# Conditioning vectors of the second layer: five of ten formed behind the expert slots, their weights loaded during the slots

## The reference

```
mod = silu(c) @ wmod                      # c: 4 x 512, wmod: 512 x (6*512)
sa, ca, ga, sb, cb, gb = six parts of mod, each 4 x 512
ga, gb = sign(g) * max(|g|, 0.25)
x = x + ga * attn(layernorm(x) * (1 + ca) + sa)
x = x + gb * ffn (layernorm(x) * (1 + cb) + sb)
```

## Time and profile before

| | us |
|---|---|
| median of 3 runs (1924.27 to 1926.55) | 1926.1 |
| the profiled execution, its own time | 1928.25 |
| its span, first to last instruction | 1925.8 |
| TensorE busy in the span | 1798.4 (93%) |
| VectorE | 1179.9 (61%) |
| ScalarE | 754.3 (39%) |
| GpSimd | 688.0 (36%) |
| chain that ended last: TensorE, VectorE, DMA, GpSimd | 68%, 12%, 6%, 3% |

### The profile page before, as it was taken

The page is one execution under the profiler, slowest core; times in us unless marked ns, Lnnn a source line. Parts: engine busy times, 40 slices in busy tenths (PEclk is TensorE's granted clock), DMA queues, the critical chain, the costliest instruction groups (busy, mean ns, idle before and its releaser), DMA issues.

```text
span 1925.8 us, 25658 instructions
## 1 busy us (share of the span) xinstructions
PE 1798.4 (93%) x8308; PEld 1406.5 (73%) x8308; DVE 1179.9 (61%) x2152; ACT 754.3 (39%) x1465; POOL 688.0 (36%) x678
## 2 busy tenths in 40 slices
PE   8889999999999999998799999679799999999995
PEld 5556788888888888876566777468688787787784
DVE  5556676666666766677763344556557466575654
ACT  2534455554555555543622222266622213222120
POOL 1335222112222212211253556634536436344442
PEclk9999999999999999999989999889999999999998
DMA  6122353535352544622377998710001101001011
GB/s 246 45 91 82 119 160 92 177 109 197 100 191 81 169 137 142 203 74 75 132 247 216 277 276 222 155 70 26 23 24 50 33 6 55 27 9 51 6 55 44
DMA packets 99905, 216.33 MB, mean 112 GB/s; under 512 B 8456, under 2 KB 33048, under 8 KB 98288
## 3 DMA queue, kind: packets, MB, share of 16 engines
q1 hardware_dynamic: 77696, 166.60, 26.6%
q0 software_dynamic: 11520, 28.96, 6.4%
q10 hardware_dynamic: 10608, 19.74, 3.3%
HBM read 123.93 MB, written 91.35 MB: 112 GB/s over the span
## 4 chain that ended last, share of the span: by engine, by line
PE 68%; DVE 12%; issue 7%; DMA 6%; POOL 3%; ACT 3%; POOLq 0%; ACTq 0%; DVEq 0%; SPq 0%
PE bank L770 19%; PE bank L772 18%; PE bank L771 18%; DMA u_d<-yt,sm 4%; PE bank L1011 2%; PE bank L874 2%; PE bank L1156 2%; DVE hh L2219 2%; PE bank L957 2%; DMA gbt<-mod_rows_d,sm 1%; POOL gbt L2450 1%; DVE rr L1906 1%; PE bank L1018 1%; DVE fl L2197 1%; PE bank L959 1%
## 5 line engine op out<-in xcount | busy, mean ns | idle before, releaser
L1906 DVE RECIPROCAL rr<-rr 128x256 f32<-128x256 f32 x128 | 218.9, 1731 | 0.0
L770 PE MATMUL bank<-hT,W1b 128*128 128x512 f32 x512 | 208.0, 406 | 7.5 <-DVE hh L2172 7.5
L770 PE MATMUL bank<-W1a,hT 128*128 128x512 f32 x512 | 209.8, 410 | 3.4 <-DVE hT L1818 3.4
L771 PE MATMUL bank<-hT,W1b 128*128 128x512 f32 x512 | 203.3, 397 | 0.0
L772 PE MATMUL bank<-hT,W1b 128*128 128x512 f32 x512 | 203.1, 397 | 0.0
L772 PE MATMUL bank<-W1a,hT 128*128 128x512 f32 x512 | 201.5, 394 | 0.0
L771 PE MATMUL bank<-W1a,hT 128*128 128x512 f32 x512 | 200.7, 392 | 0.0
L2305 POOL TENSOR_TENSOR x<-x,tmp 128x512 f32<-128x512 f32 x64 | 101.3, 1583 | 271.5 <-DVE tmp L1898 271.5
L2172 DVE TENSOR_TENSOR hh<-hh,bank 128x512 f32<-128x512 f32 x64 | 43.4, 687 | 196.5 <-PE bank L772 168.5
L1931 DVE SCALAR_TENSOR_TENSOR kt<-bank,kt 128x256 fp32r<-128x256 f32 x128 | 50.8, 397 | 162.4 <-ACT vt L1373 162.2
L2239 POOL TENSOR_TENSOR W<-stage,W 128x1024 fp32r<-128x1024 f32 x32 | 77.1, 2408 | 184.5 <-ACT W L1235 182.2
(11 more groups left out here) (272 smaller groups left out, 4467.4 us busy)
## 6 DMA issues: line engine op xcount, KB each, us to landing
hs_d<-bor SPq DMA_DIRECT2D x24, 1548.0 KB, 11.1
ws_d<-W SPq DMA_DIRECT2D x48, 512.0 KB, 6.1
WB<-ws_d SPq DMA_DIRECT2D x8, 3072.0 KB
stage<-wa SPq DMA_DIRECT2D x32, 512.0 KB
stage<-wbe SPq DMA_DIRECT2D x24, 512.0 KB
stage<-wdn SPq DMA_DIRECT2D x24, 512.0 KB
mw<-wmod SPq DMA_DIRECT2D x10, 1024.0 KB, 4.8
hg<-hs_d ACTq DMA_DIRECT2D x39, 258.0 KB
```

The lines of the kernel that those rows point to most:

```text
L770: pe.matmul(o, lhs(HI), rhs(HI), start=start, stop=False, **kw)
L771: pe.matmul(o, lhs(HI), rhs(LO), start=False, stop=False, **kw)
L1906: dve.reciprocal(rr[:, pair, h], rr[:, pair, h]).then_inc(r_rec, 1)
```

## The change

Parts 5 to 9 of `MOD_PARTS` leave the first head group, with their loads, products, copies, column groups and the last gate. Their weights get a buffer of their own, `lw`, of 5 x 2048 words from word 6144 on: its first two parts lie ahead of WB, the last three in WB's first buffer. SP issues the five loads behind that of the last expert, the last three of them after the last slot of expert 5. After the last slot TensorE forms the products in five free banks, ScalarE copies the rows and the columns (between and behind the diagonals), and GpSimd makes and stores the gate in step b=0 of stage C. ScalarE's scaling of (2, 1) goes behind the output of (2, 0).

```diff
-MOD_PARTS = [(0, GAT), (0, SB), (0, CB), (0, GBT), (1, GAT), (1, SA), (1, CA), (1, SB), (1, CB), (1, GBT)]
-MOD_FINISH = [(0,), (3,), (4,), (9,)]
-MOD_PLACE = [(0, 0), (0, 1), (0, 2), (1, 0), (1, 2), (2, 0), (2, 1), (2, 2), (3, 0), (3, 2)]
+MOD_PARTS = [(0, GAT), (0, SB), (0, CB), (0, GBT), (1, GAT)]
+MOD_FINISH = [(0,), (3,), (4,), ()]
+MOD_PLACE = [(0, 0), (0, 1), (0, 2), (1, 0), (1, 2)]
+LATE_PARTS, LATE_ROW, LATE_BANK = [SA, CA, SB, CB, GBT], [0, 1, 2, 3, 1], [0, 1, 4, 5, 7]
...
+        def over_late(a):
+            return a("before_lw", [P, 6144]), a("lw", [P, len(LATE_PARTS), NC * H])
...
+            def late_load(i):
+                if i == 2:
+                    end = sp.value_load(tab[0:1, TAB_END, GE - 3:GE - 2], min_val=1, max_val=SLOTS)
+                    sp.wait_ge(w_all, 16 * GE)
+                    sp.wait_ge(dn_full, end)
+                sp.dma_start(lw[:, i, :], wmod1[LATE_PARTS[i]]).then_inc(lw_loaded[i], 16)
...
-                    for i in ((1, 2, 3), (4, 5), (6, 7, 8), (9,))[b]:
+                    for i in ((1, 2, 3), (4,), (), ())[b]:
                         mod_load(i)
...
                 for e in range(4, GE):
                     load_expert(e)
+                for i in range(len(LATE_PARTS)):
+                    late_load(i)
...
+            def late_product(i):
+                pe.wait_ge(lw_loaded[i], 16)
+                if LATE_BANK[i] == 7:
+                    pe.wait_ge(y_evac, SLOTS - 1)
+                mod_product(bank[LATE_BANK[i]], lw[:, i, :], 1).then_inc(lm_full, 1)
+
+            def late_columns(i):
+                pe.wait_ge(lm_row, i + 1)
+                mod_columns(bank[LATE_BANK[i]], prow[:, LATE_ROW[i], :]).then_inc(lc_full, 1)
+
             def back():
+                for i in range(3):
+                    late_product(i)
+                late_columns(0)
+                late_product(3)
+                late_columns(1)
+                late_product(4)
+                late_columns(2)
+                late_columns(3)
                 for half in range(2):
                     ln_transposes((2, 0), half)
...
                 if b == 0:
+                    pe.wait_ge(lm_row, len(LATE_PARTS))
+                    pe.wait_ge(lc_done, 4)
...
+                elif (k, b) == (2, 0):
+                    act.wait_ge(lc_done, 4)
...
                     for c in range(NC):
                         act.activation(dg[:, b, HI, c, :], ident[:, :], ACT.Copy, scale=gcol[:, c, b:b + 1]) \
                             .then_inc(dg_hi, 1)
+                    if b < 3:
+                        late_row(b)
+                late_modc(0)
+                late_row(3)
+                late_modc(1)
+                late_row(4)
+                late_modc(2)
+                late_modc(3)
                 ln_scaled(2, 0)
-                ln_scaled(2, 1)
                 ln_out((2, 0), 0)
                 ln_out((2, 0), 1)
+                ln_scaled(2, 1)
+
+            def late_row(i):
+                act.wait_ge(lm_full, i + 1)
+                if i == 4:
+                    act.wait_ge(lc_full, 2)
+                act.activation(prow[:, LATE_ROW[i], :], bank[LATE_BANK[i]][0:NB, :], ACT.Copy).then_inc(lm_row, 1)
+
+            def late_modc(i):
+                kind = COL_KIND[1, LATE_PARTS[i]]
+                act.wait_ge(lc_full, i + 1)
+                columns = bank[LATE_BANK[i]][:, 0:NC * NB].rearrange("p (c b) -> p c b", c=NC)
+                act.activation(modc[:, 2 + kind // 2, kind % 2, :, :], columns, ACT.Identity,
+                               bias=ones[:, 0:1] if kind % 2 else 0.0).then_inc(lc_done, 1)
...
+            def late_gate():
+                v = prow[:, LATE_ROW[4], :]
+                pool.wait_ge(lm_row, len(LATE_PARTS))
+                gate(v)
+                pool.dma_start(rows_d[R_GB1], v).then_inc(row_stored[R_GB1], 16)
...
                 for c in range(1, NC):
                     ln_chunk(C_LNS[b], c)
+                if b == 0:
+                    late_gate()
```

More of the change, by code:

```diff
@@ L321, in over_diag @@
             return a("before_dg", [P, 8208]), a("dg", [P, NB, 2, NC, P], F32R)
-        (hT, hF, (hg, hts, sgs, pps, at, tab, sm), (_, mst), (_, WB), (W1a, W2, _, W1b), (_, xw), (_, mw, prow), (_, x0),
+        (hT, hF, (hg, hts, sgs, pps, at, tab, sm), (_, mst), (_, lw), (_, WB), (W1a, W2, _, W1b), (_, xw), (_, mw, prow), (_, x0),
          (_, h1), (_, dg)) = shared(
-            [lambda a: a("hT", [P, 2, NC, NB * S], F32R), lambda a: a("hF", [P, NC, NB * S]), over_hT, over_lo, over_both,
+            [lambda a: a("hT", [P, 2, NC, NB * S], F32R), lambda a: a("hF", [P, NC, NB * S]), over_hT, over_lo, over_late,
+             over_both,
              *map(second, (weights, over_w2, over_mods, over_x0, over_h1, over_diag))])
@@ L401, in build @@
         SIGN, ROW_A, GATE1, ROW_B = range(4)
-        ROW_OF = [ROW_A, ROW_B, None, ROW_B, GATE1, ROW_A, ROW_B, None, None, ROW_A]
-        FREED_BY = {(1, SA): R_GA0, (1, CA): R_GB0}
+        ROW_OF = [ROW_A, ROW_B, None, ROW_B, GATE1]
         mod_row = [colrow[:, :] if r is None else prow[:, r, :] for r in ROW_OF]
@@ L432, in build @@
         nw_loaded = sem("norm_w_loaded")
+        lw_loaded = [sem(f"late_part_loaded{i}") for i in range(len(LATE_PARTS))]
+        lm_full = sem("late_part_full")
+        lm_row = sem("late_part_row_copied")
+        lc_full = sem("late_columns_full")
+        lc_done = sem("late_columns_copied")
         gw_loaded = sem("router_weights_loaded")
@@ L1146, in step_c @@
                     if n < 2:
-                        pe.wait_ge(ring_read, ln_at(2, 0, 2 + n) + 1)
+                        pe.wait_ge(ring_read, ln_at(2, 0, 2 + (n + RING[("ln", 2, 0, 1)]) % 2) + 1)
                     else:
@@ L1262, in ln_out @@
                 elif k == 1:
-                    act.wait_ge(ring_done, RING[("mod", 8, "col")] + 1)
+                    act.wait_ge(ring_done, RING[("mod", 2, "col")] + 1)
+                elif (k, b) == (2, 0):
+                    act.wait_ge(lc_done, 4)
                 if n0 > 0:
@@ L1390, in step_a @@
                 if b == 1 and not (first or last):
-                    for stored in row_stored:
-                        act.wait_ge(stored, 16)
+                    for kind in (R_GA0, R_GB0, R_G1, R_R1):
+                        act.wait_ge(row_stored[kind], 16)
                     split_e(g, 0)
@@ L1847, in mod_evac @@
                         continue
-                    before = FREED_BY.get(MOD_PARTS[i])
-                    if before is not None:
-                        dve.wait_ge(row_stored[before], 16)
                     dve.wait_ge(ring_read, n)
@@ L2368, in mod_rows @@
                     pool.wait_ge(ring_done, RING[("mod", i, "col" if MOD_PARTS[i] in COL_KIND else "row")] + 1)
-                    if kind == R_GB1:
-                        pool.wait_ge(row_stored[R_R1], 16)
-                    if kind in (R_GA0, R_GB0, R_R1, R_GB1):
+                    if kind in (R_GA0, R_GB0, R_R1):
                         gate(v)
@@ L2442, in slots @@
             def slots():
-                gates = rows_d.rearrange("k b n -> (k b) n")
+                gates = rows_d[0:R_GB1].rearrange("k b n -> (k b) n")
                 def gather_gates(i):
@@ L2526, in step_d @@
                     ln_out((3, 3), 1)
+                    pool.wait_ge(row_stored[R_GB1], 16)
                     split_d(0, 4)
```

## The result

| | before | after |
|---|---|---|
| median, 20 runs each | 1926.13 us | 1920.12 us |
| ratio, 95% interval | | 0.997 (0.9959 to 0.9981) |
| the profiled execution, span | 1925.8 | 1918.2 |

What follows compares the result with a forecast made beforehand. It took TensorE to bound the first group, with VectorE part of b=2, and GpSimd's gathers and adds the late slots. Terms -7.9 - 13.2 + 4.0 - 1.0 = -18.1 took 1926.1 to 1908.0 us, range 1901 to 1917.

Steps and rivals of the forecast that it cites:

- Steps b=3 and b=2, -7.9 and -13.2: First head group: time saved, in us, as TensorE loses five products and four column groups there.
- the replay up to the tail's start: Step b=2, first group: VectorE and TensorE timelines replayed without the removed work, putting the group's output product at 129.7.
- From there I take step b=1's pattern: Step b=2: the tail starts 6.0 us after the last accumulation at 123.7, as in b=1 without its third product.
- the bound of 10: Step b=2: smallest gain, if TensorE's new stalls on VectorE cost clock; shrinking by less would show the forecast wrong.
- Rival C: First group bound by VectorE or GpSimd's weight splits, not TensorE; half of 21.1 gained, 1918 us, chance 0.09.
- Slots, +4.0: Five late loads lengthen GpSimd's wait for adds at 1190.27 by 3.9 us and the one at 1209.54 by 0.1.
- rival B: Slots: both add waits, at 1190 and 1209, fall under load traffic; +8.2, 1912.2 us, chance 0.20.
- Rival D: Slots: gathers slowed by the loads bind and cost 29 us, making the kernel slower, 1933 us, chance 0.04.
- Order on ScalarE, -1.0: Start of stage C: scaling (2, 1) behind the outputs of (2, 0) gains between 0 and 4 us, taken as 1.0.
- Late work in the gap, 0: Behind the slots: 20.3 us of late TensorE work fits the 22.38 us gap and ScalarE's copies are covered, costing nothing.
- late gate, 0: Stage C: the gate's 8 us on GpSimd delay some work by about 4 but cost nothing, at most 3.
- SP and GpSimd in group 1, 0: First group: GpSimd's earlier gate and weight split and SP's queue cost nothing, under 2 us if cover fails.

Runs made afterwards that it cites:

- e1: Kernel after without its late part (no late loads, products, copies, column groups or gate): 1908.6 us, ratio 0.9911 to before.
- e2: Kernel after without its late work, but with the five 1 MB loads kept where the change puts them: 1917.1 us, ratio 0.9954 to before.
- e10: Kernel after with the five late loads cut in 0.5 MB halves, one issued per slot from the 26th of 39 slots: 1913.6 us, ratio 0.9931 to before.
- e5: Kernel after with ScalarE's scaling of (2, 1) back ahead of the outputs of (2, 0): 1921.0 us, ratio 0.9981 to before.
- e4: Kernel after with the late gate's five GpSimd operations spread over layernorm chunks of stage C's steps b=0 and b=1: 1920.9 us, ratio 0.9975 to before.
- e11: Kernel after with first tail tile ahead of kvb's low parts, useless products in the gap, other bank for stage C's first tile: 1913.2 us, ratio 0.9930 to before.
- e12: Kernel after with the three edits of e11 plus the late loads in halves, one per slot: 1913.2 us, ratio 0.9939 to before.
- e6: Kernel after with six useless matmul pairs on TensorE in the gap behind the slots: 1918.8 us, ratio 0.9967 to before.
- e3: Kernel after with VectorE's first tail tile ahead of kvb's low parts in the first group's steps b=2 and b=3: 1916.9 us, ratio 0.9954 to before.

## Why the prediction was wrong, point by point

- **Steps b=3 and b=2, -7.9 and -13.2, together -21.1.** Measured -15.8. The products and waits that go, and the replay up to the tail's start (129.55, forecast 129.7), were right. The step that failed is "From there I take step b=1's pattern": in b=1 the third product stands ahead of the tail and covers VectorE's wait for ScalarE's kvb; in b=2 and b=3 nothing does any longer. The text had such stalls as the bound of 10 for b=2 and did not look at which instruction stands in front in VectorE's queue. Between the products with the state, b=2 came to -9.7 (47.4 to 37.7), just past the bound of 10 that was named as a sign of being wrong, and b=3 to -6.2 in place of -7.9. Rival C (half of 21.1) was the nearer picture in kind, not in size.
- **Slots, +4.0.** Measured +6.3 in the two profiles, 7 to 9 by e1 and e2. That the boundary wait behind the last expert's load would fall under traffic was right; its size, taken as 9.53 less 5.65, was not. The traffic is denser than the sum had it: the last three loads came 19.8 us behind the last expert's (forecast 23.7), and all 8 MB were through 39 us behind it (1185; forecast 46.7). A single expert's load was the nearest row, but before, no five further loads lay beside it. The second boundary, at 1209.54 before, stayed free of them (one wait of 2.18 at 1205.53). So of rival B (+8.2, chance 0.20) the size is nearly right and the place is not: the price fell on one wait and one gather. The sum also took it that TensorE stays ahead by its buffers; it was held 4.96 and came onto the chain. Rival D (the gathers bind) did not decide, but it named the way: one slow gather, not twelve, held VectorE, and by it TensorE. The Trainium skill, DMA: Bandwidth & Descriptors, section Queues, rings and completion order, says that each DMA engine changes between its queues a packet at a time, from which the prediction had worked out a term above 4. The trace agrees in the sign; that the length of the runs matters no run shows, that loads in halves and paced cost less, e10 shows.
- **Order on ScalarE, -1.0.** Measured +1.1 from the reload to the end of stage C. The order by itself is worth -2.7 (e5), more than forecast; the other bank for the first tile and the longer half clock took it back. The ring's new count was read in the diff as an index and not as a wait; the clock was not in the sum at all.
- **Late work in the gap, 0; late gate, 0; SP and GpSimd in group 1, 0.** Right as far as is shown: e2 against after, e4, and the 87.9 of e11 and e12, which leave at most 0.9 for the third.
- The sum of the three misses in the profile, 5.3 + 2.3 + 2.1, with 0.8 of spread elsewhere, is the whole distance between 18.1 and 7.6. The range took in one or two of them, not all three with one sign. By the medians the distance is 12.1; the 1.6 between 7.6 and 6.0 is less than single runs spread.

## What to carry to other kernels

When work leaves an engine's queue, look at what stood behind it in the *other* engines' queues: the product of b=2 was also the cover of a wait on VectorE, and one instruction's place was worth 2.4 to 4 us. A load that is moved beside a chain of waited-for DMAs costs what that chain waits longer, and less if it is cut and paced than if it is queued whole. Look at every engine that such a chain feeds: here one late gather put TensorE on the chain for 41 us. A gap on TensorE that is nearly filled but not quite can leave the clock at half for the following stage: read the granted clock behind it, and count waits on shared banks anew when their number of uses changes.

## What the runs showed of the hardware

- TensorE's granted clock was 1.00 until 1247 after, with 0.81 us of work in the 4 us from 1243 on, then 0.50 until 1261 although TensorE was busy 8.50 of 12 us from 1249. With the six useless pairs of e6 put into its idle time it stayed at 1.00 throughout, over remaining gaps of up to 2.1 us. What sets the moment of its return (3 us into stage C before, 7.4 after, 5.1 in e5) was not tried. Nor does the same wait always lower it: behind the wait of 2.57 us in b=2 it fell in e3 and stayed up in after, e11 and e12.
- A VectorE addition with both inputs in SBUF took 5.61 us in after and 5.58 in e3, where GpSimd had hardly a gap from 1276.73 to 1291.8, and 0.76 where the gate was spread (e4) or left out (e1). The Trainium skill, SBUF — State Buffer, section SBUF: two separate sides, says that a VectorE operation with two SBUF inputs and a GpSimd operation that reads SBUF share one port pair, which the one that starts first holds for its whole instruction. The trace agrees in kind, but the wait here spans four of GpSimd's instructions (1286.76 to 1291.8), not one.
- Five loads of 1 MB cost the stretch of the last adds 7 to 9 us when queued as two and three whole ones, and 3 to 5 when issued as halves, one per slot.
